# A norm, state-space and expert-layer kernel on Trainium2: sixth projection ahead of the counts, a counting mask of minus ones, tile planes on VectorE, row numbers read from PSUM

## The reference

```python
mod = (silu(c) @ wmod).reshape(4, 6, 1, 128)        # sa, ca, ga, sb, cb, gb
h = layernorm(x) * (1 + ca) + sa
x = x + ga * clip(h + out_proj(ssm(in_proj(norm(h)))), -10, 10)
h = layernorm(x) * (1 + cb) + sb
x_flat = h @ W_proj + b_proj                         # N = 4096 tokens, D = 128
expert = argmax(softmax(x_flat @ W_gate))            # E = 8 experts, top 1, weight 1
# each expert takes at most 2 * N / E = 1024 tokens, in token order
hid = gelu(layernorm(tok @ W1[e] + b1[e]) * g + b)   # 512 wide
out[tok] = hid @ W2[e] + b2[e]
x = x + gb * layernorm(out)
```

## Time and profile before

| | |
|---|---|
| median of 3 runs | 300.12 us (299.92 to 300.75) |
| profiled execution, its own time | 300.46 us |
| its span | 297.6 us |
| PE busy | 256.1 us (86%) |
| DVE busy | 219.5 us (74%) |
| POOL busy | 190.5 us (64%) |
| ACT busy | 150.2 us (50%) |

### The profile page before, as it was taken

How to read it: one execution, slowest core, us unless ns; L and a number is a source line. 1 busy time by engine, 2 the same in 40 slices (tenths; PEclk the granted TensorE clock), 3 DMA queues, 4 the chain that set the end, 5 groups by cost and what they waited for, 6 DMA issues and landing times.

```text
span 297.6 us, 6458 instructions
## 1 busy us (share of the span) xinstructions
PE 256.1 (86%) x1753; PEld 167.4 (56%) x1754; DVE 219.5 (74%) x895; ACT 150.2 (50%) x381; POOL 190.5 (64%) x229
## 2 busy tenths in 40 slices
PE   0998989798699999789679999999899989999730
PEld 0554655488686678564324666566556645665520
DVE  1799996998955999878626787777767776778630
ACT  3659765582332577719204564564545454545520
POOL 2489998800480566510577488888888888887561
PEclk9999999999899999959999999999999999999985
DMA  5930189921908989972032122222322232221000
GB/s 144 232 142 1 39 231 285 278 73 46 236 7 287 277 254 303 286 223 72 2 94 91 55 87 80 81 65 76 89 79 65 70 89 80 70 70 47 29 5 0
DMA packets 47297, 35.29 MB, mean 119 GB/s; under 512 B 4566, under 2 KB 42573, under 8 KB 47146
## 3 DMA queue, kind: packets, MB, share of 16 engines
q1 hardware_dynamic: 42296, 24.71, 30.2%
q0 software_dynamic: 3744, 9.77, 11.2%
q10 hardware_dynamic: 1234, 0.53, 0.8%
HBM read 24.34 MB, written 11.08 MB: 119 GB/s over the span
## 4 chain that ended last, share of the span: by engine, by line
POOL 29%; PE 27%; DVE 21%; issue 13%; ACT 3%; DMA 3%; SPq 1%; POOLq 0%; DVEq 0%; ACTq 0%
POOL out_dram L632 11%; POOL rs L642 8%; POOL rs L513 4%; PE PS L1438 3%; DVE Wst L1236 3%; DVE Wst L1225 3%; POOL SBk L624 3%; PE PS L1526 3%; PE PS L1411 2%; PE PS L1407 2%; DMA CP<-in_L_attn_C_param_dram 2%; DVE V L1219 2%; PE PS L1360 2%; PE PS L1509 2%; PE PS L1370 2%
## 5 line engine op out<-in xcount | busy, mean ns | idle before, releaser
L825 ACT ACTIVATE V<-PS,gb1T 128x128 f32<-128x128 f32 x156 | 58.8, 457 | 56.9 <-PE PS L1517 56.9
L624 POOL DMA_INDIRECT SBk<-rows,idgi x39 | 41.8, 1072 | 11.1 <-issue 7.7
L1219 DVE TENSOR_SCALAR V<-PS,mv,rs 128x512 f32<-128x512 f32 x39 | 31.5, 807 | 22.2 <-POOL rs L642 21.8
L1526 PE MATMUL PS<-BIG,V 128*128 x312 | 43.9, 283 | 3.4 <-DVE Wst L1225 1.8
L632 POOL DMA_INDIRECT out_dram<-Wst,idsi x39 | 39.7, 1017 | 11.1 <-DVE Wst L1236 7.4
L1526 PEld LDWEIGHTS PS<-BIG,V 128*128 128x128 f32 x312 | 41.5, 197 | 5.0 <-issue 4.5
L1509 PE MATMUL PS<-BIG,V 128*128 x78 | 40.6, 602 | 2.6 <-issue 2.6
L642 POOL TENSOR_TENSOR rs<-ve,half 128x2 f32<-128x2 f32 x42 | 30.5, 725 | 10.5 <-DVE ve L1240 9.6
L1209 DVE BATCH_NORM_STATS2 st<-PS 128x6 f32<-128x512 f32 x39 | 27.0, 693 | 6.2 <-PE PS L1511 5.8
L1517 PE MATMUL PS<-ident,V 128*128 128x128 f32 x156 | 25.6, 286 | 0.9 <-DVE V L1219 0.6
L589 POOL TENSOR_TENSOR Hh<-Hh,outb 128x1024 f32<-128x1024 f32 x4 | 9.5, 2402 | 19.5 <-ACT SBk L746 19.5
(11 more groups left out here) (256 smaller groups left out, 544.0 us busy)
## 6 DMA issues: line engine op xcount, KB each, us to landing
BIG<-k_pad SPq DMA_DIRECT2D x32, 256.0 KB, 5.6
X<-in_L_attn_x_dram SPq DMA_DIRECT2D x4, 512.0 KB, 6.8
BIG<-in_L_ffn_W_dram SPq DMA_DIRECT2D x1, 2048.0 KB, 9.7
rows<-GL SPq DMA_DIRECT2D x4, 512.0 KB, 5.0
rows<-Hh SPq DMA_DIRECT2D x8, 256.0 KB, 4.5
out_dram<-Hh SPq DMA_DIRECT2D x8, 256.0 KB, 4.2
rows<-U SPq DMA_DIRECT2D x4, 512.0 KB, 4.1
Wst<-la_rows SPq DMA_DIRECT2D x1, 1024.0 KB, 4.7
```

What stands on the lines that cost most here:

```text
L624: pool.indirect_dma_start(out=XG[:, u, :], out_offset=None, in_=rows, in_offset=bass.IndirectOffsetOnAxis(ap=idgi[:, t:t + 1], axis=0), bo ...
L825: a.activation(AT[:, u, k, :], PS[:, 3, P * k:P * k + P], ACT.Gelu, bias=gb1T[:, 1, bass.ds(e, 1), k], scale=gb1T[:, 0, bass.ds(e, 1), k]) ...
L1219: v.tensor_scalar(NH[:, w, :], PS[:, w, :], mv1[:, w, 0, 0:1], rs1[:, w, 0:1], ALU.subtract, ALU.mult).then_inc(s_nh, 1)
L1526: m.matmul(dst, AT[:, u, k, :], W2s[:, bass.ds(e, 1), k, :].rearrange("p a d -> p (a d)"), start=(k == 0), stop=False)
```

## The change

- TensorE, early part: `project(6)` stands ahead of `counts(0)` and of the last unit's transposes; one `fill` (two products) stands behind these.
- The counting mask holds -1 at and behind a token's position and 0 elsewhere, so that rank minus total comes from one product; columns are ordered by expert. The copy of the totals and one subtraction go in the first range, the subtraction in the second.
- GpSimd no longer makes the OT plane by tile: VectorE makes both. VectorE no longer makes the last chunk of OR: ScalarE makes chunks 0, 1 and 3, with its two planes by row placed between.
- `idgi` is made first, from PSUM, and releases the gathers by itself; `idsi` follows.
- Ahead of the expert loop each tile's `up` stands ahead of the next tile's `rows_in`.
- In the last rounds, tile 38's `turn` stands ahead of tile 37's `down` (after a wait for all gelus of tile 37), and VectorE finishes tile 37's rows ahead of the sums of tile 38's.

```diff
-        lower = sb("lower", [P, P], BF16)
+        notabove = sb("notabove", [P, P], BF16)
...
+            step.mark(g.memset(notabove[:], 0.0))
...
-            g.affine_select(out=lower[:], in_=onesb[:], pattern=[[1, P]], compare_op=ALU.is_gt, fill=0.0,
+            g.affine_select(out=notabove[:], in_=notabove[:], pattern=[[1, P]], compare_op=ALU.is_gt, fill=-1.0,
...
-            for n, half_t in enumerate(HALVES):
-                pool.wait_ge(s_ot, n + 1)
-                g.tensor_tensor(OT[:, half_t, 1, :], OT[:, half_t, 0, :],
-                                bc(tiota_b[:, half_t].unsqueeze(2), [P, NT // 2, MAX_TILES]),
-                                ALU.mult).then_inc(s_ott, 1)
-
-            pool.wait_ge(s_idx, 1)
-            pool.wait_ge(s_xf, 16 * 4 * B)
-
             last_row = pool.alloc_register("last_row")
             pool.reg_mov(last_row, N - 1)
...
+            pool.wait_ge(s_xf, 16 * 4 * B)
+            pool.wait_ge(s_idx, 1)
...
                 if t == 0:
+                    pool.wait_ge(s_idx, 2)
                     pool.wait_ge(s_pre, 16 * 2 * B)
...
+            act.wait_ge(s_rown, 1)
+            distances(0)
+            distances(1)
+            near(0, 1)
+            near(1, 2)
+            act.wait_ge(s_rown, 2)
+            distances(NT // OHC - 1)
+            by_row(0)
+            near(NT // OHC - 1, 3)
+            by_row(1)
...
-                totals = PS[:, 2 * k + 1, 0:n * E].rearrange("p (t e) -> p e t", e=E)
-                step.mark(v.tensor_copy(tot[k], totals))
-                step.settle()
+                totals = PS[:, 2 * k + 1, 0:n * E].rearrange("p (e t) -> p e t", e=E)
                 if k:
+                    step.mark(v.tensor_copy(tot, totals))
+                    step.settle()
...
-                step.mark(v.tensor_tensor_scan(flat(inc[k]), flat(seg[k][:]), flat(tot[k]), 0.0, ALU.mult, ALU.add))
+                    totals = tot
+                step.mark(v.tensor_tensor_scan(flat(inc[k]), flat(seg[k][:]), flat(totals), 0.0, ALU.mult, ALU.add))
...
-                step.mark(v.tensor_tensor(pos[k], inc[k], totals, ALU.subtract))
-                step.settle()
-                step.mark(v.tensor_tensor(pos[k], pos[k], rank, ALU.add))
+                back = PS[:, 2 * k, 0:n * E].rearrange("p (e t) -> p e t", e=E)
+                step.mark(v.tensor_tensor(pos[k], inc[k], back, ALU.add))
...
+                v.tensor_scalar(rown[:, rng], rowi[:, rng], -1.0, None, ALU.mult).then_inc(s_rown, 1)
                 if k == 0:
-                    v.tensor_scalar(rown[:, rng], rowi[:, rng], -1.0, None, ALU.mult).then_inc(s_rown, 1)
-                v.tensor_copy(rowb[:, rng], rowi[:, rng]).then_inc(s_row, 1)
+                    v.tensor_copy(rowb[:, rng], rowi[:, rng]).then_inc(s_row, 1)
...
-            dve.wait_ge(s_row, 2)
-            for c4 in range(ACT_OHC + 1, NT // OHC):
-                row_onehots(c4).then_inc(s_ohd, 1)
+                dve.wait_ge(s_ot, n + 1)
+                v.tensor_tensor(OT[:, half_t, 1, :], OT[:, half_t, 0, :],
+                                bc(tiota_b[:, half_t].unsqueeze(2), wide), ALU.mult).then_inc(s_ott, 1)
...
+            found, tile_of, row_of = (PS[:, 5, MAX_TILES * c:MAX_TILES * c + MAX_TILES] for c in range(3))
+            step.mark(v.tensor_copy(idf, row_of))
+            step.settle()
+            v.scalar_tensor_tensor(idgi[:], tile_of, float(P), idf, ALU.mult, ALU.add).then_inc(s_idx, 1)
+            step.mark(v.tensor_scalar(ids, found, -float(2 * N), float(2 * N), ALU.mult, ALU.add))
+            step.settle()
+            dve.wait_ge(s_idx, 1)
+            v.tensor_tensor(idsi[:], ids, idgi[:], ALU.add).then_inc(s_idx, 1)
...
+                rows_late = static and t == MAX_TILES + RING - 1
+                if rows_late:
+                    token = XG[:, (k - RING - 1) % XRING]
+                    dve.wait_ge(s_sc[w], 16 * rounds)
+                    v.scalar_tensor_tensor(FO[:, w, :], PS[:, 5 + w, 0:D], mv1[:, w, 1, 0:1], token[:, 2 * D:3 * D],
...
+                if n >= 1 and early:
+                    project(n - 1)
                 if n == 2 * B - 1:
                     counts(0)
                 if early:
                     rows_turn2(n)
-                if n >= 1:
+                    fill(4, MOD[:, 0].rearrange("p b d -> p (b d)"), 1)
+                if n >= 1 and not early:
                     project(n - 1)
...
+                final = static and t == MAX_TILES - 1
+                if final:
+                    pe.wait_ge(s_a, KC * t)
+                    turn(t, u)
                 if not static or t >= 1:
                     down(t - 1, (u - 1) % RING, e[k], static and t - 1 < RING)
-                turn(t, u)
+                if not final:
+                    turn(t, u)
...
-            pe.wait_ge(s_idx, 1)
+            pe.wait_ge(s_idx, 2)
...
             for t in range(2):
-                pe.wait_ge(s_xt, t + 1)
+                up(t, t, e[t + 1])
                 rows_in(t + 1, t + 1, 1)
-                up(t, t, e[t + 1])
```

More of the change, by code:

```diff
@@ L794, in _, with distances @@
                     turned2(n)
-            act.wait_ge(s_rown, 1)
-            for c4 in range(ACT_OHC):
+            def distances(c4):
                 for t in range(OHC * c4, OHC * c4 + OHC):
@@ L1221, in expert_step @@
                 token = XG[:, (k - RING - 1) % XRING]
-                if final:
+                if final and not rows_late:
                     if rounds is not None:
```

49 lines of the change are left out of this document (22 added, 27 removed).

## The result

The changed kernel took **296.55 us** (median of 4 runs, 296.22 to 296.94), the kernel before 300.44 us beside it (4 runs, 299.92 to 301.92): a ratio of 0.9871, 95% interval 0.9834 to 0.9908. Forecast were 296.9 us and a gain of 3.25 us; the gain was 3.9 us, and the time lies inside the forecast's own range (296.0 to 298.2 us). The profiled execution took 296.94 us with a span of 294.9 us, so 2.04 us lie around the span (2.86 us before).

A forecast was written before the change was run, and what follows sets the result against it. A chain of waits through GpSimd, TensorE and VectorE bounds the kernel, no engine owning the span. Terms: -3.3 (T) - 0.6 (row numbers) + 0.65 (products) + 0 (end) = -3.25 us, 300.12 to 296.9; own range 296.0 to 298.2, full 295.9 to 299.3.

The forecast's parts named there:

- Part 1: TensorE's early stage, sixth projection ahead of counting products: clock stays at 2.4 GHz, ScalarE free at 131.25 instead of 134.59 us.
- Part 2: VectorE's first range, mask of minus ones and no totals copy: scan 0.5 us instead of 1.52, gain 1.25 us.
- Part 3: From the second assignment to the tile numbers, one 64-column operation goes (0.2 us): 7.05 us instead of 7.29.
- Part 4: Planes on VectorE, last row one-hots on ScalarE: ScalarE last, one-hot products end (T) at 144.2 us, gain 3.3 us.
- Part 5: Row numbers from PSUM: first transpose 5.2 us after the one-hot products' end, behind the fillers, 0.6 us gained.
- Part 6: Ahead of the expert loop, products before next transposes: first product sooner, first gelu 0.65 us later (0.3 to 0.9).
- Part 7: At the end, last tile's transposes ahead of the previous tile's product: worth 0 (-0.3 to +0.3 us).
- (a): Rival: TensorE's clock falls in the early stage all the same, ScalarE free 2.4 us later, 299.3 us; chance 0.05.
- (d): Rival: low clock lasts through two stretches, from the fillers through the first three tiles, 303 us; chance 0.04.
- (b): Rival: clock falls in the wait ahead of the one-hot products, costing 2.4 to 3.4 us, 299.3 to 300.3; chance 0.15.
- c: Rival: through the port, VectorE's scan and multiplication stay slow, 297.6 to 298.3 us; chance 0.1.
- e: Rival: VectorE's two multiplications or ScalarE's longer list eat the gain, T as before, about 300 us; chance 0.03.

The follow-up runs named there:

- Experiment 2: The changed kernel with TensorE's old early order (counting products before the sixth projection) and no filler pair: 300.0 us, ratio 1.0002 to the kernel before.
- experiment 3: The kernel before with only the change's early TensorE order (sixth projection ahead of counting products) and the filler pair: 298.59 us, ratio 0.9932.
- Experiment 6: The changed kernel with the fourth chunk of row one-hots back on VectorE and off ScalarE: 295.59 us, ratio 0.9819 to the kernel before.
- experiment 8: The changed kernel with five filler pairs instead of six ahead of the first gathered tile: single time 297.45 us.
- experiment 9: The changed kernel with the last tile's old order of TensorE and VectorE put back: 296.79 us, ratio 0.9877 to the kernel before.
- experiment 4: The changed kernel with totals copied to SBUF for the scan: 297.46 us, ratio 0.9907; with GpSimd's last addition also delayed, single time 298.45 us.
- experiment 1: Both kernels profiled and timed again without edits: changed 296.77 us (6 runs), before 300.36 us (19 runs), ratio 0.989.

## Why the prediction was right

On the time base of before (0.37 us added to the times of after):

- **Part 1, sixth projection ahead of counts: right to 0.1 us.** Unit 7's products were to end at 130.65 us and ended at 129.08 + 1.19 + 0.37 = 130.64; ScalarE free at 131.25, measured 131.24. Experiment 2 shows that the gain at the Square hangs on this step, most of it by the clock (some 2.3 of 3.3 us, an estimate), experiment 3 that it alone is worth 2.36 us there.
- **Part 2, scan and copy: right, with one term too cheap.** The scan was to take 0.5 us and took 0.55. The counting products, costed at 0 to 0.2 us and hidden, cost more: both end at 127.81 us (127.44 in the trace of after), forecast 127.45, and VectorE waited 0.24 us for them. The assignment ended at 130.91 against 131.1 us all the same, since the product with the mask, expected to start when GpSimd's addition ends and to take 0.51 us from there, ended 0.37 us behind that end. The two errors cancel in part.
- **Part 3: right.** 130.54 to 137.56 us are 7.02 us, forecast 7.05.
- **Part 4: right, in the engine as well.** The multiplication cost 0.81 us, not the 1.95 us of GpSimd; VectorE ended at 141.15 (forecast 141.4), ScalarE last at 142.90 (143.05), T = 144.00 (144.2). The gain at T was 3.47 us, forecast 3.3. Experiment 6 shows what that imbalance costs: 1.07 us. But parts 1 to 3 brought all of this gain, and part 4 nothing. With the planes still on GpSimd its multiplications would have started 0.89 us behind VectorE's first comparison, as before, and taken 3.90 us: 137.56 + 0.89 + 3.90 = 142.35 us, where ScalarE's last plane ended at 142.53 (an estimate, in the times of after; no run takes the planes alone back). The forecast's own numbers say the same, 138.15 + 0.89 + 3.90 = 142.94 against 143.05 us. The planes on VectorE gained about as much as the chunk on ScalarE cost.
- **Part 5: right.** The transpose came 5.04 us behind T (forecast 5.2), held by the fillers; the landing at T + 4.85 us, as forecast, is shown by experiment 8. The gather started 0.91 us behind the end of `idgi`, as forecast.
- **Part 6: the right sign, mis-sized.** "0.65 us later (0.3 to 0.9)" was reckoned from the 5.61 us of the old order. The spacing of the new order came out well (6.42 us, forecast 6.25), and against the kernel before the first gelu comes 0.81 us later behind the first transpose, inside the bounds. But the old order would itself have become shorter in this kernel, 5.40 us, so that the step costs 1.02 us, beyond the upper bound. This is the term that was mis-sized.
- **Part 7: right where the clock stays up.** Worth 0; experiment 9 gives 0. The forecast looked at the queues alone. That TensorE's new wait of 1.73 us can bring the clock down (0.4 to 1.0 us in four profiles of nine) was not in it.
- **The sum.** At the first gelu -3.44 us (34.98 to 31.54), forecast -3.25: the order -2.36, scan and copy -0.99, planes -0.12, row numbers -0.78, first products +0.81. These are differences of stages in this sequence of kernels: of the order's 2.36 us only 2.0 would have reached T with the planes on GpSimd (experiment 3). The medians moved by -3.9 and -3.6 us in the two comparisons. At the end the first profiles alone would have said -2.4 us, and with it the forecast's sign of being wrong, "if GpSimd's last queue moves": from the first gelu to the last power it took 1.03 us more than before. That was the one execution of before with the short lag; its second profile has 127.26 us and the first of after 127.21. So the forecast's number was met by stages that came out close, with errors of 0.1 to 0.2 us of either sign at T, at the fillers and at the first products.

**The rivals.** The clock falling early (a) and in both stretches (d) were not seen with the changed kernel. The clock falling ahead of the one-hot products (b) didn't come in the two profiles of the changed kernel, but it did in one of the order alone, and one such stretch stood ahead of an expert product with the scan from SBUF. So the mechanism exists, but b's price of 2.4 to 3.4 us rested on a low stretch of 6.9 us, and these two were shorter: 4 x (1 - 0.57) x 2 = 3.4 us in the order alone, 6 x (1 - 0.72) x 2 = 3.4 us with the scan from SBUF (mean clock 0.72 from 151 to 157 us). They cost 0.70 and 1.08 us. In the changed kernel, where the transpose stands behind the fillers, the stretch of the order alone would cost its fillers' 0.82 us as well, 1.5 us together (an estimate). c (scan and multiplication stay slow) is refuted by the 0.55 and 0.81 us above; experiment 4 puts the Square 0.61 us later with the scan slow and its copy back, near c's 0.65 us for the scan alone. e (no gain) is refuted by the ratio.

**The chances.** They don't add up as written: the forecast, c and all of a are 0.63 + 0.10 + 0.05 = 0.78, not 0.8 with "a little of a", and b, most of a and e are some 0.22, not 0.16.

**Open.** What decides in a single execution whether TensorE's transposes trail GpSimd's power by 1.6 or by 2.8 us was not settled. Nor was how often the clock falls in the short waits, ahead of the one-hot products and of the last tile's transposes: each kernel has one or two profiles. The price of the clock apart from the order, and the planes apart from the chunk, are estimates.

## What to carry to other kernels

Where a low clock sits on the path, look for what TensorE waited for just ahead of it, and put work that is ready in that wait; a shorter VectorE operation is worth nothing until that is done (experiments 2 and 3), and then each microsecond counts again. After work has moved between engines, look once more at which engine ends last: here the freed one could have kept the chunk (1.07 us), and without that the move bought nothing, by the estimate above. Getting the first item out sooner isn't the aim if it delays the last item that the loop waits for (1.02 us). And a reordering that is worth nothing on the queues isn't free if it opens a wait in front of TensorE (1.73 us at the last tile).

## What the runs showed of the hardware

- **Strided columns.** The counting product of 192 bf16 columns took 0.24 us with its moving operand read in order, 0.50 us read with a step of eight elements (16 bytes), which puts the second of the pair 0.32 us behind the first and not 0.08 to 0.09. Order and clock are not the reason: in the order alone, at the same place and at 1.00, it took 0.25 us. The Trainium skill (SBUF — State Buffer, Door 1: The DMA port swizzle) says that SBUF has lines of 16 bytes and that each access to a new line pays; each column is a new line here, and the trace agrees.
- **A fall of the clock in short waits is not certain.** In the changed kernel waits of 1.75 and 0.71 us stood ahead of the two halves, and the clock stayed at 1.00; in the order alone waits of 1.51 and 1.15 us stood there, and it fell; in the kernel before waits of 1.53 and 1.15 us, and 1.51 and 1.14 us in its second profile, stood there, and it stayed at 1.00. Behind the wait of 1.73 us ahead of the last tile's transposes it fell in four profiles of nine. The stretch from 78 to 84 us, in which neither kernel differs, was low in nine of the fourteen profiles and not in the other five, and where it wasn't the last norm came some 1.6 us sooner (124.4 to 124.9 against 126.0 to 126.5 us). Times from such profiles can be compared only from a common instruction on. The timed executions are mixed in the same way: of the 19 of the kernel before in experiment 1, eight have spans of 296.3 to 297.1 us and ten of 298.4 to 298.9 us; that it is this stretch that divides them is likely and not shown.
